# Layer norm statistics joined on GpSimd instead of VectorE, in a gated attention and expert kernel

## The reference

```python
def _layernorm(x, axis=-1, eps=1e-05):
    m = jnp.mean(x, axis=axis, keepdims=True)
    v = jnp.var(x, axis=axis, keepdims=True)
    return (x - m) / jnp.sqrt(v + eps)

x = x + jnp.tanh(g_xattn[0]) * _L0_xattn_ref(_layernorm(x), ctx_1024, mask, Wq, Wk, Wv, Wo, bo)
x = x + jnp.tanh(g_ffn[0])   * _L0_ffn_ref(_layernorm(x), gate_w, gate_up_w, down_w)   # 8 experts, top 2
x = x + jnp.tanh(g_xattn[1]) * _L1_xattn_ref(_layernorm(x), ctx_1024, ctx_1024, ...)
x = x + jnp.tanh(g_ffn[1])   * _L1_ffn_ref(_layernorm(x), w_freq_real, w_freq_imag, bias)  # Fourier
```

## Time and profile before

| | before |
|---|---|
| median of three runs | 1391.45 us |
| the profiled execution | 1391.23 us |
| its span, first to last instruction | 1389.5 us |
| TensorE busy | 1220.1 us (88%) |
| VectorE busy | 896.5 us (65%) |
| ScalarE busy | 579.5 us (42%) |
| GpSimd busy | 287.6 us (21%) |
| mean granted TensorE clock | 0.955 of full speed |

### The profile page before, as it was taken

The page is one execution under the profiler, slowest core; times in us unless marked ns, Lnnn a source line. Parts: engine busy times, 40 slices in busy tenths (PEclk is TensorE's granted clock), DMA queues, the critical chain, the costliest instruction groups (busy, mean ns, idle before and its releaser), DMA issues.

```text
span 1389.5 us, 34876 instructions
## 1 busy us (share of the span) xinstructions
PE 1220.1 (88%) x11942; PEld 1019.9 (73%) x11943; DVE 896.5 (65%) x2615; ACT 579.5 (42%) x1232; POOL 287.6 (21%) x474
## 2 busy tenths in 40 slices
PE   1799999997499999899998999999976899999996
PEld 1587878875378878688787887778863777777784
DVE  3588888886265665655656565565545777777773
ACT  3465665664132422423323242322223556555663
POOL 2034454432300000000000000000013344444410
PEclk9899999998789999999999999999996999999999
DMA  6234343334530130310302112000112222222210
GB/s 208 85 116 132 130 130 124 115 98 141 196 122 30 34 117 30 113 31 29 121 30 79 64 60 91 30 31 30 43 37 70 61 85 72 66 76 83 73 40 23
DMA packets 78987, 112.87 MB, mean 81 GB/s; under 512 B 27394, under 2 KB 47623, under 8 KB 76886
## 3 DMA queue, kind: packets, MB, share of 16 engines
q1 hardware_dynamic: 62550, 59.76, 13.7%
q0 software_dynamic: 10624, 41.95, 9.1%
q10 hardware_dynamic: 5760, 10.49, 2.0%
HBM read 64.54 MB, written 40.89 MB: 76 GB/s over the span
## 4 chain that ended last, share of the span: by engine, by line
PE 59%; issue 21%; DVE 12%; ACT 2%; POOL 2%; DMA 2%; SPq 1%; DVEq 0%; another core or an unknown queue 0%; POOLq 0%; ACTq 0%
PE bank L1612 18%; PE bank L1625 8%; PE bank L1414 6%; PE bank L1463 5%; PE bank L1339 4%; PE bank L1359 3%; PE bank L1392 3%; PE bank L1390 2%; PE bank L1450 2%; DVE we L1267 2%; DVE bm L1021 2%; PE bank L1416 2%; PE bank L1372 1%; PE bank L1461 1%; PE bank L1366 1%
## 5 line engine op out<-in xcount | busy, mean ns | idle before, releaser
L1612 PE MATMUL bank<-tiles,we 128*128 128x256 f16 x3456 | 428.7, 279 | 23.0 <-issue 20.2
L1612 PEld LDWEIGHTS bank<-tiles,we 128*128 128x128 f16 x3456 | 343.1, 100 | 79.9 <-issue 33.6
L893 ACT ACTIVATE tiles<-bank 128x256 f32<-128x256 f32 x288 | 110.4, 383 | 382.1 <-PE bank L1612 382.1
L1277 DVE SCALAR_TENSOR_TENSOR tiles<-bank,tiles 128x256 f32<-128x256 f32 x288 | 121.9, 423 | 219.4 <-ACT tiles L893 218.7
L1625 PE MATMUL bank<-we,tiles 128*128 128x256 f16 x1728 | 233.0, 274 | 15.3 <-DVE tiles L1281 14.4
L1625 PEld LDWEIGHTS bank<-we,tiles 128*128 128x128 f16 x1728 | 162.1, 98 | 49.9 <-DVE tiles L1281 27.3
L1414 PE MATMUL bank<-qT,kbd 128*128 128x256 f16 x960 | 150.3, 275 | 5.7 <-ACT pr L762 2.7
L1021 DVE TENSOR_REDUCE bm<-bank 128x4 bf16<-128x308 f32 x256 | 116.5, 474 | 57.4 <-PE bank L1392 50.5
L1283 DVE TENSOR_TENSOR tiles<-tiles 128x256 f16<-128x256 f32 x288 | 122.6, 426 | 10.0 <-DVE tiles L1281 0.2
L430 DVE TENSOR_TENSOR pr<-pr 128x512 f16<-128x512 f32 x160 | 108.6, 683 | 31.1 <-ACT pr L762 28.5
L1414 PEld LDWEIGHTS bank<-qT,kbd 128*128 128x128 f16 x960 | 92.7, 99 | 24.0 <-ACT pr L762 3.7
(11 more groups left out here) (184 smaller groups left out, 1794.3 us busy)
## 6 DMA issues: line engine op xcount, KB each, us to landing
expert_out<-zeros SPq DMA_DIRECT2D x16, 768.0 KB
tiles<-expert_in SPq DMA_DIRECT2D x37, 256.0 KB, 2.6
wes<-in_guT POOLq DMA_DIRECT2D x9, 1024.0 KB, 5.1
expert_out<-tiles ACTq DMA_DIRECT2D x36, 256.0 KB, 2.0
pr<-in_guT POOLq DMA_DIRECT2D x7, 1024.0 KB
yg<-in_dnT POOLq DMA_DIRECT2D x7, 1024.0 KB
xin<-in_x SPq DMA_DIRECT2D x16, 256.0 KB
xb<-in_x SPq DMA_DIRECT2D x16, 256.0 KB
```

What stands on the lines that cost most here:

```text
L893: act.activation(ge[:, fc % 2], bank[1 + fc % 3][:, 0:S], ACT.Gelu, scale=INV).then_inc(s.gelu, 1)
L1277: dve.scalar_tensor_tensor(a32[:, fc % 2], bank[1 + fc % 3][:, S:2 * S], INV, ge[:, fc % 2], ALU.mult, ALU.mult).then_inc(s.product, 1)
L1612: last = pe.matmul(bank[1 + fc % 3][:, half * S:(half + 1) * S], gate_up[:, par, c, i, col:col + P], xT[:, j, c], start=n == 0, stop=n == 5)
```

## The change

`bn_aggr` and the filler between the statistics operations go from VectorE, and so do `renorm` and `pre_norm`. `stats` is now two `bn_stats`, ahead of which VectorE waits until the shift of the batch before has been made (`query_scale`, `after_shift`), since `st` is read by GpSimd. On GpSimd `ln_root` gives way to `moments`, which joins the two halves that `bn_stats` leaves, and to a last operation or two:

```diff
-            def ln_root(kind, count, done, b):
-
-                ch = Chain(pool, (s.root_step, s.root_after_step)[kind], 1, b.n)
-                wait_apart(pool, done, b.n + 1)
-                ch.link(pool.tensor_scalar(ve[:, kind], mv[:, kind, :, 1], EPS, 1.0, ALU.add, ALU.mult))
-                pool.tensor_tensor(rstd[:, kind], ve[:, kind], mhalf[:], ALU.pow).then_inc(count, 1)
+            def moments(kind, done, b):
+
+                ch = Chain(pool, (s.root_step, s.root_after_step)[kind], 6 - kind, b.n)
+                halves = st[:, kind].rearrange("p t (h k) -> p t h k", h=2)
+                pool.wait_ge(done, b.n + 1)
+                pool.tensor_tensor(both[:, kind], halves[:, :, 0, 1:3], halves[:, :, 1, 1:3], ALU.add)
+                ch.link(pool.tensor_tensor(apart[:, kind], halves[:, :, 0, 1], halves[:, :, 1, 1], ALU.subtract))
+                pool.tensor_tensor(square[:, kind], apart[:, kind], apart[:, kind], ALU.mult)
+                pool.tensor_scalar(within[:, kind], both[:, kind, :, 1], 1.0 / D, EPS, ALU.mult, ALU.add)
+                ch.link(pool.tensor_scalar(shift0[:, kind], both[:, kind, :, 0], -0.5, None, ALU.mult))
+                ch.link(pool.tensor_tensor(spread2[:, kind], square[:, kind], quarter[:], ALU.mult))
+                ch.link(pool.tensor_tensor(ve[:, kind], spread2[:, kind], within[:, kind], ALU.add))
+                ch.link(pool.tensor_tensor(rstd[:, kind], ve[:, kind], mhalf[:], ALU.pow))
+                return ch
+
+            def norm_after(b):
+                ch = moments(1, s.variance_after, b)
+                pool.tensor_tensor(nr[:], shift0[:, 1], rstd[:, 1], ALU.mult).then_inc(s.after_shift, 1)
+                ch.end()
...
             def root(b):
-                ln_root(0, s.root, s.variance, b)
+                ch = moments(0, s.variance, b)
+                pool.wait_ge(s.mask_step, 4 * NB + 3 if b.layer else 4 * b.n + 3)
+                if not (isinstance(b.n, int) and b.n < 1):
+                    pool.wait_ge(s.normed, b.n)
+                ch.link(pool.tensor_tensor(rq[:], rstd[:, 0], nf[:], ALU.mult))
+                pool.tensor_tensor(nq[:], shift0[:, 0], rq[:], ALU.mult).then_inc(s.query_scale, 1)
+                ch.end()
...
             pool.memset(cell[0:1, 1:2], 0.0).then_inc(s.pool_setup, 1)
+            pool.memset(quarter[:], 0.25)
...
             def stats(kind, src, sem_done, b, par):
-                ch = Chain(dve, (s.stats_step, s.stats_after_step)[kind], 1, b.n, wait_apart)
+                if not (isinstance(b.n, int) and b.n < 1):
+                    dve.wait_ge((s.query_scale, s.after_shift)[kind], b.n)
                 dve.bn_stats(st[:, kind, 0], src[:, par, 0])
-                ch.link(dve.bn_stats(st[:, kind, 1], src[:, par, 1]))
-                dve.bn_aggr(mv[:, kind, 0], st[:, kind, 0])
-                dve.bn_aggr(mv[:, kind, 1], st[:, kind, 1]).then_inc(sem_done, 1)
+                dve.bn_stats(st[:, kind, 1], src[:, par, 1]).then_inc(sem_done, 1)
...
-            def pre_norm(b, first=False):
-
-                ch = Chain(dve, s.norm_step, 1, b.n)
-                dve.wait_ge(s.root, b.n + 1)
-                if not first:
-                    dve.wait_ge(s.normed, b.n)
-                ch.link(dve.tensor_tensor(rq[:], rstd[:, 0], nf[:], ALU.mult))
-                dve.scalar_tensor_tensor(nq[:], mv[:, 0, :, 0], -1.0, rq[:],
-                                         ALU.mult, ALU.mult).then_inc(s.query_scale, 1)
...
-            def renorm(b):
-                dve.wait_ge(s.root_after, b.n + 1)
-                dve.scalar_tensor_tensor(nr[:], mv[:, 1, :, 0], -1.0, rstd[:, 1],
-                                         ALU.mult, ALU.mult).then_inc(s.after_shift, 1)
...
                 w_low(b, 2)
-                if tail:
-                    renorm(pv)
                 if pre:
                     pre_stats(b.after(2))
...
                     maxima(nx, 4)
-                if pre:
-                    pre_norm(b.after(2))
                 if front:
                     maxima(nx, 5)
```

More of the change, by code:

```diff
@@ L169, in build @@
         mhalf = sb("mhalf", [P, QT], F32)
+        quarter = sb("quarter", [P, QT], F32)
         cell = sb("cell", [1, 130], F32)
@@ L199, in build @@
         st = sb("st", [P, 2, QT, 6], F32)
-        mv = sb("mv", [P, 2, QT, 2], F32)
+        both = sb("both", [P, 2, QT, 2], F32)
+        apart = sb("apart", [P, 2, QT], F32)
+        square = sb("square", [P, 2, QT], F32)
+        spread2 = sb("spread2", [P, 2, QT], F32)
+        within = sb("within", [P, 2, QT], F32)
+        shift0 = sb("shift0", [P, 2, QT], F32)
         ve = sb("ve", [P, 2, QT], F32)
@@ L289, in build @@
         s.variance = sem("variance")
-        s.root = sem("root")
         s.variance_after = sem("variance_after")
-        s.root_after = sem("root_after")
         s.base_even = sem("base_even")
@@ L349, in build @@
         s.mask_step = sem("mask_step")
-        s.norm_step = sem("norm_step")
         s.attended_step = sem("attended_step")
-        s.stats_step = sem("stats_step")
-        s.stats_after_step = sem("stats_after_step")
         s.root_step = sem("root_step")
@@ L648, in step @@
                 if tail:
-                    ln_root(1, s.root_after, s.variance_after, pv)
+                    norm_after(pv)
                 if pre:
@@ L669, in _ @@
             steps(pool, 0, step)
-            ln_root(1, s.root_after, s.variance_after, at(0, 15))
+            norm_after(at(0, 15))
             for i in (14, 15):
@@ L698, in _ @@
             steps(pool, 1, step)
-            ln_root(1, s.root_after, s.variance_after, at(1, 15))
+            norm_after(at(1, 15))
         @block.scalar
@@ L1193, in _ @@
             mask_flags(at(0, 0))
-            pre_norm(at(0, 0), True)
             mask_rows(at(0, 0), True)
@@ L1202, in _ @@
             mask_flags(at(0, 1))
-            pre_norm(at(0, 1))
             mask_rows(at(0, 1))
@@ L1208, in _ @@
             residual(at(0, 15))
-            renorm(at(0, 15))
             route(at(0, 15))
@@ L1316, in _ @@
                     dve.tensor_copy(nfb[:], nf[:].unsqueeze(2).to_broadcast([P, QT, 2])).then_inc(s.unmasked_ready, 1)
-                    pre_norm(at(1, 0))
             v_low(at(1, 0))
@@ L1324, in _ @@
                 maxima(at(1, 0), g)
-            pre_norm(at(1, 1))
             combine(at(1, 2))
@@ L1328, in _ @@
             residual(at(1, 15))
-            renorm(at(1, 15))
             finish(at(1, 15))
```

## The result

The changed kernel takes 1409.03 us (median of 4 runs, 1402.02 to 1411.45) against 1392.16 us of the kernel before beside it (4 runs): 1.0122 times as long, 95% interval 1.0094 to 1.0150. Forecast were 1396.0 us and a range that ended at 1406. The profiled execution has a span of 1405.7 us against 1389.5, so 16.2 us more, and these can be placed.

| part | before | after | difference |
|---|---|---|---|
| start to the residual of batch 0, first pass | 68.37 | 67.85 | -0.5 |
| stretches 0 to 12, first pass | 240.72 | 237.31 | -3.4 |
| stretch 13, first pass | 18.90 | 21.13 | +2.2 |
| stretch 14, first pass | 17.72 | 19.82 | +2.1 |
| rest of the pass, experts, opening of the second pass | 745.49 | 745.70 | +0.2 |

The account below looks back on a forecast made before the run. TensorE, working 94 of 100 us, was taken as the bound. Exposed places +7.9, second-pass opening -0.3 and first-pass steady steps -2.8 gave +4.8 us on 1391.2: 1396.0 us, range 1384 to 1406.

Parts of the forecast that it names:

- GpSimd's chain: Norm chains on GpSimd: after-norm shift about 1.0 us later in steady steps, just fitting 1.15 us slack, cost nothing.
- Rival 2: After-norm chain too long: shift 1.5 us later, 0.35 us beyond slack in each of 27 steps, 1406 us; chance 0.18.
- Rival 3: GpSimd holds up VectorE's residue operations: 0.4 us a step in the first pass, +5.6, 1402 us; chance 0.07.
- VectorE's gain: First pass's steady steps: VectorE's freed time saves 0.2 us a step over 14 steps, -2.8 us; second pass 0.
- Rival 1: VectorE was the real bound: gains 0.7 us a first-pass step and 0.3 a second-pass step, 1385 us; chance 0.25.
- The exposed places: Six places where TensorE waits for a norm: four after-norms, two query norms, batch 14's extra; together +7.9 us.
- batch 14: Last full step of each pass: after-norm 1.14 us later, plus 0.6 us for GpSimd running beside residue operations.
- The gathers: Second pass: gathers 2 us later on GpSimd; `combine` waits up to 0.6 us where VectorE waits for ScalarE anyway; cost 0.
- The landing of 1.9 us: Time for gathered data to land, read at the second pass's start, 1040.39 to 1042.29.
- The slack of 1.4 us: Second-pass steady step: 3.3 us from last gather's end to `combine`'s read, less landing, set against 2 us of delay.

Follow-up runs that it names:

- e14: Changed kernel without the second pass's gathers of batches 3 to 15 and their waits: 1355.65 us, 1.0056 times the kernel before, chip two.
- e13: Kernel before without the second pass's gathers of batches 3 to 15 and their waits: 1348.44 us, 1.0003 times the kernel before, chip two.
- e10: Changed kernel with two of four gathers ahead of the after-norm's chain and the exposed norms as before: 1370.04 us, 0.9847 times the kernel before, chip one.
- e12: Changed kernel, gathers split, exposed norms as before, plus 32 zero matmuls before each pass's last transposes: 1362.84 us, 0.9800 times the kernel before, chip one.
- e11: Kernel before with two of the four second-pass gathers issued ahead of its norm chains: 1379.43 us, 0.9924 times the kernel before, chip one.
- e9: Changed kernel with 24 zero matmuls on TensorE ahead of h2's transposes in each pass's last step: 1404.97 us, 1.0093 times the kernel before, chip one.
- e1: Kernel before with the change in the first pass alone: 1351.31 us, 1.0019 times the kernel before, chip two.
- e18: Kernel before with the change in the first pass alone, run again: 1351.82 us beside 1349.57, one run, chip two.
- e3: Changed kernel without the second pass's gathers of batches 3 to 15 and their waits: 1362.62 us, one run, chip two.
- e6: Changed kernel run again, against the kernel before: 1375.70 us, 1.0201 times, chip two.
- e7: Changed kernel with two of the four second-pass gathers issued ahead of the after-norm's chain: 1355.89 us, 1.0060 times the kernel before, chip two.
- e8: Changed kernel with after-norms of batches 14 and 15 and each pass's first query norm as before: 1366.02 us, 1.0127 times the kernel before, chip two.
- e5: Kernel before, unchanged, profiled again: 1348.44 us, chip two.
- e15: Kernel before with 13 one-element GpSimd operations ahead of the second pass's gathers, run again: 1362.25 us, 1.0101 times the kernel before, chip two.
- e2: Kernel before with 13 one-cell GpSimd fillers ahead of each second-pass step's gathers: 1362.82 us, 1.0108 times the kernel before, chip two.
- e4: Kernel before without the second pass's gathers of batches 3 to 15 and their waits: 1344.09 us, one run, chip two.
- e16: Kernel before without the second pass's gathers of batches 3 to 15, run again: 1348.75 us beside 1349.57, one run, chip two.
- e17: Kernel before with its second-pass gathers held back by GpSimd fillers, run again: 1365.05 us beside 1349.57, one run, chip two.

## Why the prediction was wrong

- **GpSimd's chain, right.** Its busy time rose from 287.6 to 372.1 us (forecast: 80 or more). In the steady stretches the norm is ready just in time: four waits of TensorE for `h2_norm`, no more. Rival 2 didn't happen, though the time it gave, 1406, was the nearest. Rival 3 neither, since e14's steady stretches equal e13's. The Trainium skill, "SBUF — State Buffer", section "Who interferes with whom", has a VectorE instruction with two SBUF inputs and a GpSimd instruction that reads SBUF exclude each other; the blocked addition and square (0.56 and 0.54 us, 0.20 and 0.19 when alone) agree, and the residues stayed at 0.68 to 0.69 us in the mean of 160, so here GpSimd alone paid.
- **VectorE's gain: the direction right, the size not shown.** -2.8 us forecast for the first pass's steady steps, -3.4 measured on chip one. But e10 and e12, with the same norm in these stretches, took 240.04 and 238.47 us there, more than the 237.31 of the changed kernel and about what the two with the norm as before take (240.72, and 239.51 in e11). In each of these profiles the granted clock falls in some of the stretches, and the late release has moved. Chip two gives the gain cleanly: 225.0 to 225.2 us in seven profiles with the moved norm, 226.6 to 226.7 in seven without, so 1.5 us. Rival 1 didn't happen.
- **The exposed places: the mechanism right, one term missing.** TensorE's waits for `h2_norm` grew from 12.1 to 17.7 us (forecast "about 18") and those for `h_norm` from 41.9 to 44.6 (44). For batch 14 the forecast had 1.14 + 0.6 = 1.7 us; e9 shows 2.0. But +7.9 us was only the sum of the waits. The clock added 3.9 us in stretch 14 of the second pass (e9); the forecast never asked what TensorE's longer idle time does to the work behind it.
- **Stretch 13 of the first pass: not the norm.** It grew by 2.2 us in the profile though it was counted as steady. In e1, whose first pass is the changed one, it took 18.41 us at a granted clock of 1.00, within what the kernel before takes at that clock (18.25 to 18.90); e14 and e18 took 18.77 and 18.68, and e10 and e12 on chip one 19.1. Where the clock was at 0.50 once, it took 19.85 to 20.85 us with the moved norm (e3, e6, e7, e8, e9) and 19.02 to 19.79 with the old one (e5, e11, e15); in the changed kernel of the prediction the clock fell twice. The windows of the stretch in e1 and in the changed kernel, the granted clock third from the end:

```profile
292.30:310.71 18.41, 15.57 (x188) 13.01 (x186) 14.28 (x42) 11.64 (x20) 6.92 (x15) 1.00 0.47 160
```

```profile
305.16:326.29 21.13, 18.04 (x187) 15.10 (x185) 14.65 (x43) 11.64 (x20) 7.57 (x15) 0.84 0.41 139
```

- **The gathers: the step that failed.** "`combine` waits up to 0.6 us, at a point where VectorE next waits for ScalarE anyway; cost 0." Three things in it were wrong. The landing of 1.9 us was read from the pass's opening; in steady stretches it takes 2.0 to 2.6 (e6). The slack of 1.4 us was read from a stretch of chip one, where `combine` itself comes late; on chip two it is negative, as the 0.39 us wait in e5 shows. And the cover behind `combine` was never added up: it is some 1 us, and the next residual is the fifth operation behind it. The term was put at 0; the twelve stretches show 8.7 us on chip one and 17.4 on chip two, of 29.8 in all there, and e2, e7 and e14 show it from three sides.
- **The same on chip one.** Here `combine` waits only 2.2 us for its gathers outside the opening, about as forecast, yet the twelve stretches lose 8.7 us. Of these, 3.3 lie in stretches 2 and 7, where the granted clock fell once each (0.92 in the mean), and 5.4 in the other ten; in e9, the same code, the clock fell in five of the twelve, and they took 5 us more. The 5.4 come with the late release under the gathers, which has the normalisation start about 1 us later. That the gathers' place decides is shown: e11 changes nothing but the place of two of them and wins 11.6 us, and e10's second-pass stretches are 26 us below the changed kernel's. Why TensorE's results are released late is not. In the four kernels of chip one that I read, the late release falls into the time in which GpSimd issues gathers (6.8 to 11.9 us behind the residual in the kernel before, 9.1 to 14.0 in the changed one; in e11 two go out up to 9.3 us and two from 17 us on, around the next residual), and in e10, where two go out between 8.7 and 11.1 us and two around the next residual, it has nearly gone. Stretches 12 and 13, which issue no gathers, show none of it on chip one either: in the kernel before the turn is read at 7.7 to 7.8 us behind the residual and the normalisation starts at 12.4 to 12.5, as on chip two; but they have no `combine` either. And in the first pass it moves with the scatter, as shown above. But no run that only leaves the gathers out reached that chip, and chip two issues the same transfers at the same places without a late release, so this is a coincidence in time and not a cause that was tested.
- **Also open.** Between the first pass's last residual and the second pass's first there are 3.7 us more in e6 than in e5 and 0.2 more on chip one; some is the exposed norm of batch 15, some lies in the experts, whose code is the same in both and which varied by 2 to 5 us among these runs; the kernel before alone took 736.1 to 739.9 us there on chip two. e10 and e12 were not run on chip two; there the two repairs were only measured singly, 19.8 and 9.7 us below the changed kernel, which took 26.5 more than the kernel before.

## What to carry to other kernels

When an engine's in-order queue gets a longer chain, cost everything issued behind it up to its last reader, and for that reader add up the idle time in its own queue until the next thing that everyone waits for; "it waits there anyway" needs a number. Where a chain grows on an engine that issues transfers, issue the transfers ahead of the chain, in the time in which it waits for its input: here that was worth 20 us of 1376 (e7), and 12 of 1391 in the kernel before (e11). Where TensorE already stands idle, as in the last stretch of a pass here, more idle time costs its length and can cost the work behind it at half the clock (1.4 to 4.1 us in this kernel), so leave exposed places as they were, or fill them with matmuls nobody reads. And before a longer stretch is put down to a change, look at its granted clock, and at the same stretch in other runs.

## What the hardware showed that was not expected

- The granted clock fell from 1.00 to 0.50 while TensorE idled for 3.00 us in e6. At the same place in the kernel before, with 1.01 us, it stayed at 1.00 in the profiles of the kernel before, e4, e5, e13 and e15, but fell later in the same stretch in e2, e16 and e17.
- The kernel before differs by 3% between chips: spans of 1389.5 and 1346.7 us. 34.8 of the 42.8 us lie in the steady stretches (240.72 against 226.60 and 236.11 against 215.45). On chip one only, results of TensorE are read up to 1.5 us (first pass) and 3.5 us (second pass) after the recorded end of its matmuls. Also on chip one only, the clock falls in some of the steady stretches, in four of the first pass of the kernel before (0.91 in the mean of each).
- An indirect gather of 128 rows takes 0.95 to 1.1 us of GpSimd's time in most cases, with 0.30 us between two of them, so four hold it for 4.8 to 5.3 us, and in e6 their data is there 2.0 to 2.6 us after the last.
